# A two-layer graph network on one core: stores of normalised rows moved to ScalarE's queue, an addition moved under the last attention head, and expert numbers read in two places

## What is computed

```
x = x + gat(layernorm(x))     # graph attention, 12 heads of 64, output through relu
x = x + moe(layernorm(x))     # gate picks 1 of 4 experts (768 -> 384 -> gelu -> 768)
x = x + gcn2(layernorm(x))    # two graph convolutions 768 x 768
x = x + ffn(layernorm(x))     # 768 -> 384 -> gelu -> 768
```

## Time and profile before

| quantity | value |
|---|---|
| time, median of 3 runs | 1161.73 us (1159.79 to 1162.33) |
| time of the profiled execution | 1162.42 us |
| its span, first to last instruction | 1160.6 us |
| mean granted TensorE clock | 0.958 of full speed |
| PE, DVE, ACT, POOL busy | 1019.8, 640.9, 272.7, 53.0 us |
| moved by DMA | 65.18 MB, mean 56 GB/s |

### The profile page before, as it was taken

One profiled execution on the slowest core, in us unless ns is written; L12 is line 12 of the kernel. 1 busy time (PEld: TensorE's weight loads), 2 busy tenths in 40 slices (PEclk: granted clock), 3 DMA queues, 4 the chain that ended last, 5 costly groups with the idle time before them and its releaser, 6 DMA issues. The chain is left out here.

```text
span 1160.6 us, 17194 instructions
## 1 busy us (share of the span) xinstructions
PE 1019.8 (88%) x5932; PEld 817.5 (70%) x5932; DVE 640.9 (55%) x1360; ACT 272.7 (23%) x708; POOL 53.0 (5%) x107
## 2 busy tenths in 40 slices
PE   0596999979999999996718999399999999999996
PEld 0595666659999999995515666266699656887884
DVE  3336999979999999996822222365211111423330
ACT  0233111144444644431301110012111111301010
POOL 1000000000000000001211221100000000000000
PEclk9997999989999999998868999699999999999999
DMA  2001000000001000122841222431510000300001
GB/s 104 37 1 49 1 0 0 0 1 23 23 22 43 22 22 23 42 94 83 320 182 52 82 95 77 174 129 54 178 44 1 1 0 10 124 27 20 21 17 52
DMA packets 23867, 65.18 MB, mean 56 GB/s; under 512 B 4065, under 2 KB 7917, under 8 KB 23689
## 3 DMA queue, kind: packets, MB, share of 16 engines
q1 hardware_dynamic: 21736, 54.28, 12.8%
q0 software_dynamic: 2080, 10.23, 2.6%
HBM read 47.74 MB, written 16.76 MB: 56 GB/s over the span
## 5 line engine op out<-in xcount | busy, mean ns | idle before, releaser
L707 PE MATMUL O<-X,masks 125*125 125x264 f32 x1200 | 280.5, 333 | 4.1 <-DVE masks L844 4.1
L704 PE MATMUL O<-X,CSR 125*125 125x132 f32 x1080 | 245.4, 227 | 0.0
L707 PEld LDWEIGHTS O<-X,masks 125*125 125x125 f32 x1200 | 222.6, 188 | 4.3 <-issue 4.3
L844 DVE SCALAR_TENSOR_TENSOR masks<-a2b,NA,CSR 125x375 fp32r<-125x375 f32 (+1 forms) x360 | 213.0, 651 | 13.2 <-PE O L707 6.6
L704 PEld LDWEIGHTS O<-X,CSR 125*125 125x125 f32 x1080 | 205.2, 190 | 0.0
L556 PE MATMUL pc<-ohs,ohd 125*125 125x512 f16 (+1 forms) x660 | 130.8, 353 | 3.0 <-DVE ohs L528 3.0
L528 DVE TENSOR_SCALAR ohs<-iota,srcf 125x1250 f16<-125x1250 f16 x220 | 120.3, 547 | 0.0
L556 PEld LDWEIGHTS pc<-ohs,ohd 125*125 125x125 f16 x660 | 78.1, 138 | 53.4 <-DVE ohs L528 22.8
L1525 PE MATMUL pw<-W 128*125 128x384 f32 x240 | 81.4, 497 | 1.0 <-ACT W L1661 1.0
L1745 DVE SCALAR_TENSOR_TENSOR UL<-pw,dinv,UH 125x768 fp32r<-125x768 f32 x20 | 20.4, 1018 | 111.2 <-ACT UH L1668 111.2
L1525 PE MATMUL pw<-region,xr_or_h 128*125 128x384 f32 x240 | 77.6, 486 | 0.0
(11 more groups left out here) (213 smaller groups left out, 1279.0 us busy)
## 6 DMA issues: line engine op xcount, KB each, us to landing
a2b<-a_rows SPq DMA_DIRECT2D x12, 610.4 KB
W<-in_L_ffn_W SPq DMA_DIRECT2D x1, 4608.0 KB, 15.5
WM<-in_L_ffn_W SPq DMA_DIRECT2D x1, 4608.0 KB, 27.1
xr_or_h<-in_x SPq DMA_DIRECT2D x2, 1875.0 KB
region<-in_x SPq DMA_DIRECT2D x2, 1875.0 KB
z_rows<-region SPq DMA_DIRECT2D x10, 375.0 KB
region<-y_rows SPq DMA_DIRECT2D x10, 375.0 KB
x_rows<-xr_or_h SPq DMA_DIRECT2D x10, 375.0 KB
```

The costliest lines, as they stand in the source:

```text
L704: nc.tensor.matmul(O[0:P, bank, d - d0, 2 * DP:4 * DP], CSR[:, s, d * P:(d + 1) * P], X[:, buf, s, 4:6, :].rearrange("p k d -> p (k d)"), ...
L707: ins = nc.tensor.matmul(O[0:P, bank, d - d0, 0:4 * DP], kept, X[:, buf, s, 0:4, :].rearrange("p k d -> p (k d)"), start=s == 0, stop=s == ...
L844: nc.vector.scalar_tensor_tensor(masks[:, s, 0:(d1 - d0) * P], a2b[:, buf, d0 * P:d1 * P], NA1[:, s, bass.ds(h, 1)], CSR[:, s, d0 * P:d1 * ...
```

## The change

1. The ten stores of z are issued by ScalarE, each behind the two copies of the transposed tile, instead of by SP behind the weights.
2. `max(XR, 0) + XI` leaves the gate stage. In the attention stage VectorE does it in two instructions for the columns of heads 0 to 10 (704 columns of five node tiles each), behind the masks of the last head, and in two more for the last 64 columns after that head is combined.
3. VectorE reads four of its 13 expert numbers in the gate stage and nine in the expert stage, behind the copies of slot tile 0. TensorE reads 11 and 2, the two behind the transposition of slot tile 0. ScalarE still reads 13 in the gate stage.
4. The transposition and copy of the first expert bias (`b1r`, `b1T`) go behind the gates instead of before them.

```diff
+                def add_x(k, heads):
+
+                    for n in range(2):
+                        h = slice(n * NT // 2, (n + 1) * NT // 2)
+                        c = slice(heads[0] * DH, heads[1] * DH)
+                        dve.wait_ge(s_xi[n], 16)
+                        k.mark(nc.vector.scalar_tensor_tensor(XR[:, h, c], XR[:, h, c], 0.0, XI[:, h, c], ALU.max, ALU.add))
...
                     head(H - 1, 1, last=True)
+                    k.wait()
+                    add_x(k, (0, H - 1))
                     for step in combine(H - 1):
                         pass
+                    k.wait()
+                    add_x(k, (H - 1, H))
+                    k.wait()
...
-                    for t in range(NT):
-                        sp.wait_ge(s_z3, t + 1)
-                        sp.dma_start(z_t[:, t, :], ZA[:, t, :]).then_inc(s_zst, 16)
                     sp.wait_ge(s_gt3, NT)
                     sp.dma_start(be2[:, :, :], a["L0_ffn_b2"].partition_broadcast(128)).then_inc(s_b4, 16)
...
                     pe.wait_ge(s_eid, 1)
-                    for j in range(NS):
+                    for j in range(NS - 2):
                         experts_pe.append(expert_of(pe, j))
...
                                            ).then_inc(s_ztc3, 1)
+                        act.dma_start(z_t[:, t, :], ZA[:, t, :]).then_inc(s_zst, 16)
                         if t:
                             copy_gates(t - 1)
...
-                        if t % (NT // 2) == 0:
-                            dve.wait_ge(s_xi[2 * t // NT], 16)
-                        nc.vector.scalar_tensor_tensor(XR[:, t, :], XR[:, t, :], 0.0, XI[:, t, :], ALU.max,
-                                                       ALU.add).then_inc(s_x1, 1)
-                        dve.wait_ge(s_x1, t + 1)
                         layernorm_stats(ch, XR[:, t, :], t)
...
-                    for j in range(NS):
+                    for j in range(NS - 9):
                         experts_dve.append(expert_of(dve, j))
...
                     turn_slots(0)
+                    for j in range(NS - 2, NS):
+                        experts_pe.append(expert_of(pe, j))
...
                     copy_slots(0)
+                    for j in range(NS - 9, NS):
+                        experts_dve.append(expert_of(dve, j))
                     copy_hidden(0)
```

More of the change, by code:

```diff
@@ L969, in slowly @@
                         k.end(H)
+                    k.wait()
+                    add_x(k, (0, H))
+                    k.wait()
                 either(dve, quickly, slowly)
@@ L1049, in program @@
             s_wg, s_b1, s_b1t, s_c3 = sem("gate_w_in"), sem("moe_b1_in"), sem("moe_b1_turned"), sem("constants3")
-            s_x1, s_z3, s_zt3 = sem("x1_done"), sem("z3_ready"), sem("z3_transposed")
+            s_z3, s_zt3 = sem("z3_ready"), sem("z3_transposed")
             s_ztc3, s_g3 = sem("z3t_copied"), sem("gates_done")
@@ L1125, in turn_gates @@
                                             ident[0:NEXP, 0:NEXP]).then_inc(s_gt3, 1)
-                    pe.wait_ge(s_b1, 16)
-                    nc.tensor.transpose(pb1[:, 0:NEXP * MH], b1r[:, :], ident[0:NEXP * MH, 0:NEXP * MH]).then_inc(s_b1t, 1)
+                    turn_z(0)
                     pe.wait_ge(s_wg, 32)
-                    turn_z(0)
                     for t in range(NT):
@@ L1137, in _ @@
                     turn_gates(NT - 1)
+                    pe.wait_ge(s_b1, 16)
+                    nc.tensor.transpose(pb1[:, 0:NEXP * MH], b1r[:, :], ident[0:NEXP * MH, 0:NEXP * MH]).then_inc(s_b1t, 1)
                     pe.wait_ge(s_oh3, 1)
@@ L1155, in copy_gates @@
                         nc.scalar.copy(gT[:, t * P:(t + 1) * P], pgt[0:NEXP, t % 2, 0:P]).then_inc(s_gc3, 1)
-                    act.wait_ge(s_b1t, 1)
-                    nc.scalar.copy(b1T[:, :, :].rearrange("p e m -> p (e m)"), pb1[:, 0:NEXP * MH])
                     for t in range(NT):
@@ L1169, in _ @@
                     copy_gates(NT - 1)
+                    act.wait_ge(s_b1t, 1)
+                    nc.scalar.copy(b1T[:, :, :].rearrange("p e m -> p (e m)"), pb1[:, 0:NEXP * MH])
                     act.wait_ge(s_eid, 1)
```

## The result

The changed kernel takes 1165.83 us (median of 5 runs, 1165.38 to 1166.24); the kernel before took 1160.55 us (5 runs, 1159.79 to 1162.33). The ratio is 1.0042 with a 95% interval of 1.0027 to 1.0056, so it is slower, by 5.3 us. The profiled execution took 1165.38 us, its span 1163.6 (before 1160.6). These two traces differ by 3.0 us only: the one of before was taken 1.9 us above its median. So the traces serve for single stages here, and the medians for the whole.

The account below looks back on a forecast made before the run. Five DMA engines carrying weights, z stores and `be2`, then the gathers, were taken to bound the gate stage. Terms 0.95 + 3.7 + 0.1 gave +4.75 us: 1167.2 us profiled, 1166.5 as median, range 1149 to 1168.

Parts of the forecast that it names:

- What bounds the stage: Gate stage: five DMA engines work without a gap on weights, z stores and `be2`, 57 us, and the stores wait for these.
- The stores, +3.7 us: Gate stage: with stores on ScalarE's queue, `be2` goes ahead of the last stores, which land at 607.3 instead of 603.6.
- Rival 1: Gate stage: ScalarE's queue gets more than its turn on the five engines, stores land early, up to 13.5 us won; chance 0.38.
- The additions, +0.95: End of attention stage: the two small additions run behind the last instruction, +0.95 us (0.8 to 1.3); the large ones just fit.
- The expert numbers: Gate stage: known near 590, all engines in the barrier by 600; a full ScalarE queue delays them some 7 us, path takes 0.
- rival 3: Gate stage: a full queue stops ScalarE for long, gates come some 20 us later and set the gather, 1168 to 1172; chance 0.04.
- The reads, 0: Gate and expert stages: moving two reads on TensorE and nine on VectorE behind the barrier wins nothing and costs 0.
- The remark that their division matters once the stores are early: Gate stage: only if stores land early, by 590 at the extreme, do TensorE's 11 reads bound the barrier, at 597.7.
- The sum: Whole kernel: 0.95 for small additions, 3.7 for `be2` ahead of the stores, 0.1 for large additions, together +4.75 us.

## Why the prediction was right, and where it was not

**What bounds the stage: right.** Five DMA engines, not the queue. It was an inference from a share of 0.32 and the late landing of `be2`; putting the same stores on all sixteen took 10.4 us off the kernel before. One sum in that reading doesn't close: from about 548 us to WM2's landing at 573.95 it is 26 us for the weights and not 24, 59 in all and not 57. Nothing hangs on it, since the forecast uses only the place of `be2`.

**The stores, +3.7 us: right in mechanism, smaller in sum.** The prediction left open whether the queues share by bytes (weights landed near 593 us) or by pieces (near 599): it is by pieces, 228 to 225, and they landed at 596.8. `be2` ahead of the last stores costs 3.8 us, by the experiment that moves it behind the barrier. The gather came only 2.98 us later, since the rest of the stage is 0.84 us shorter to the gather (59.49 to 58.65). For this I have no cause: the five engines carry the same bytes. The drain was 0.3 us longer. Together 3.25 us where 3.7 was the term.

**Rival 1, the stores overtake the weights: wrong**, by 260 pieces against 259. It had 0.38 where the forecast had 0.42, so the sign was hardly called with confidence, and the range of 1149 to 1168 us was wide enough for both. The Trainium skill, "DMA: Bandwidth & Descriptors", section "Queues, rings and completion order", has an engine go round between its queues packet by packet. By that rule neither queue can win, and the trace now agrees in the equal counts.

**The additions, +0.95: mis-sized.** It measured 1.56. The work was right (0.90 us, and the large ones fit). What I did not count is the wait in front of the branch at the stage's end. Before, the branch ran beside the last combine; the change puts a wait for the last addition ahead of it, and the branch at 544.4 and the way to the barrier, where VectorE's drain starts at 545.0, then lie behind the addition. Taking that one wait out gave 0.66 us back. I had priced the added instructions and not the added wait, though the diff shows three of them.

**The expert numbers: this step failed, and its cover held.** I expected them near 590 and all engines in the barrier by 600; they came at 597.7 and ScalarE arrived at 607.4. The step said that a full queue is reached "only by the last two tiles", with some 7 us at most. Three of the last four stores were held, for 1.8, 5.0 and 10.9 us, and the numbers came 52.4 us into the stage where wide stores, which are not held, gave 42.4: 10 us. The rates were right (a tile every 2.4 us, about 5.9 us for a store that takes turns with the weights). Wrong was the count: "Some five stores would have to be outstanding". When the held issues ended, at 569.77, 575.34 and 588.29 us, the queue had sent 395, 539 and 818 of the 875, 1000 and 1250 pieces issued, so 480, 461 and 432 were left, which is less than four stores. The ninth issue took 0.35 us and left 575, so no plain count of pieces is the limit; what it is stays open. ScalarE and TensorE arrive 8 us before GpSimd's drain ends (607.4 against 615.4), so nothing of it reached the time. With 8 us more of it the change would have been rival 3.

**The reads, 0: right**, and alone they measured 0.9992 to 1.0011. The remark that their division matters once the stores are early was wrong: TensorE and VectorE with all 13 reads still arrive 0.1 us before the drain ends.

**The sum.** 1.56 + 2.98 + 0.3 = 4.8 where 4.75 was forecast. Two of the terms were off by 0.6 and -0.4 and met in the middle. That the sum fits to 0.1 us is luck; that each term has its sign and its place is not.

## What to carry to other kernels

When a stage waits for a transfer, read first on how many DMA engines it runs (its share and GB/s while it is alone), and only then which queue it stands in: another queue for the same five engines moved 3 us the wrong way, the same stores in two pieces of 112 and 13 rows gave 10. A load that nobody needs soon should be behind the one that is waited for and not beside its gathers. A wait in front of a branch or a stage's end is a cost of its own; and an engine that issues DMAs between its computing steps is held when its queue is full, here for up to 10.9 us.

## What the runs showed of the hardware

- Two queues with work on the same five engines sent equally many pieces, 260 to 259, at 130 GB/s together, the rate of one queue alone; with pieces of 1536 B against 3072 B it was still 228 to 225.
- A DMA issue on ScalarE took 0.26 us for most of the first stores and up to 10.91 us later, with between three and five earlier stores outstanding; with the stores on 16 engines no issue of twenty took more than 1.05 us, in four traces.
- GpSimd's drain behind three indirect gathers took 6.6 to 7.95 us in eleven traces, and 10.2 us when 1.5 MB of another load ran beside them.
- The first loads of x, split, kept 16 engines busy (a share of 1.04 in 8 to 20 us) but moved only 248 GB/s, where the weights' loads move 398 at 1.03. I have not tried why.
- From its first mask to its last the attention stage took 273.4 us in three traces (the first kernels with wide z stores on either queue, and the one with `be2` behind the barrier) and 274.4 to 274.9 in the others, with the same code and a granted clock of 0.99 in both groups. The account above is therefore taken from a stage's own start.
